# A mixture-of-experts tile's first weights: loaded from memory into a ring of four instead of copied on chip into a ring of three

## What is computed

```python
probs = jax.nn.softmax(x_flat @ w_gate + b_gate, axis=-1)      # 8 experts
route_p, route_idx = jnp.max(probs, axis=-1), jnp.argmax(probs, axis=-1)
h = jax.nn.relu(jnp.einsum('nd,edm->enm', x_flat, W1) + b1[:, None, :])   # 128 -> 512
y = jnp.einsum('enm,emd->end', h, W2) + b2[:, None, :]                    # 512 -> 128
out = y[route_idx, jnp.arange(n)] * route_p[:, None]
...
x = x + 0.5 * ffn(layernorm(x))
x = x + attn(layernorm(x))        # 16 heads of 8, causal
x = x + 0.5 * ffn(layernorm(x))
```

## Time and profile before

| | |
|---|---|
| runs | 321.22, 322.14, 323.71 us; median 322.14 |
| span of the profiled execution, first to last instruction | 319.3 us |
| TensorE busy | 276.5 us (87%) |
| VectorE busy | 214.5 us (67%) |
| ScalarE, GpSimd busy | 159.7 (50%), 178.8 us (56%) |
| DMA, mean over the span | 92 GB/s, 29.37 MB |
| expert tiles, first hidden product to last output product | 41.6 to 86 us and 264.4 to 309 us |

### The profile page before, as it was taken

How to read it: one execution, slowest core, us unless ns; L and a number is a source line. 1 busy time by engine, 2 the same in 40 slices (tenths; PEclk the granted TensorE clock), 3 DMA queues, 4 the chain that set the end, 5 groups by cost and what they waited for, 6 DMA issues and landing times.

```text
span 319.3 us, 7990 instructions
## 1 busy us (share of the span) xinstructions
PE 276.5 (87%) x2396; PEld 224.1 (70%) x2396; DVE 214.5 (67%) x691; ACT 159.7 (50%) x389; POOL 178.8 (56%) x319
## 2 busy tenths in 40 slices
PE   8573999999995776999999999998977699999960
PEld 8463999999994363656666566665646588999960
DVE  3877048788608759987666777776787555888850
ACT  2430076666204834586666667768541107666620
POOL 5577815554525201587777787788657730554551
PEclk9855999999999998799999999999976579999996
DMA  6973141220040731662524522110001143222100
GB/s 180 403 293 119 53 95 54 65 63 31 24 126 8 199 121 53 197 180 88 156 79 134 152 72 74 57 53 6 3 19 42 42 121 86 51 67 71 34 10 0
DMA packets 34387, 29.37 MB, mean 92 GB/s; under 512 B 4108, under 2 KB 28817, under 8 KB 34352
## 3 DMA queue, kind: packets, MB, share of 16 engines
q1 hardware_dynamic: 29696, 23.52, 24.6%
q0 software_dynamic: 2496, 4.27, 4.1%
q10 hardware_dynamic: 2160, 1.14, 1.4%
HBM read 17.08 MB, written 12.55 MB: 93 GB/s over the span
## 4 chain that ended last, share of the span: by engine, by line
PE 58%; POOL 11%; DVE 10%; issue 7%; DMA 5%; ACT 4%; POOLq 1%; ACTq 0%; SPq 0%; DVEq 0%
PE bank L1279 13%; PE bank L1290 12%; PE bank L1207 5%; PE bank L1436 3%; PE bank L1408 3%; PE bank L1384 3%; POOL pT L541 2%; POOL row L454 2%; PE bank L1381 2%; PE bank L1414 2%; PE bank L1271 2%; POOL disp_d L462 2%; PE bank L1240 2%; PE bank L1466 2%; PE bank L1389 1%
## 5 line engine op out<-in xcount | busy, mean ns | idle before, releaser
L723 ACT ACTIVATE pT<-bank 128x512 f32<-128x512 f32 x96 | 56.4, 599 | 36.2 <-PE bank L1414 25.2
L1207 PE MATMUL bank<-zero 128*128 128x128 f32 x298 | 43.2, 314 | 9.4 <-DVE rowi L916 4.7
L1279 PE MATMUL bank<-xsT,ew 128*128 128x128 f32 x368 | 48.8, 276 | 0.2
L1290 PE MATMUL bank<-experts,hT 128*128 x368 | 48.9, 276 | 0.0
L1207 PEld LDWEIGHTS bank<-zero 128*128 128x128 f32 x298 | 41.6, 227 | 10.1 <-DVE rowi L916 4.7
L1038 DVE TENSOR_REDUCE mh<-bank 128x2 f32<-128x512 f32 x64 | 42.1, 682 | 8.5 <-PE bank L1384 8.2
L541 POOL TENSOR_SCALAR_AFFINE_SELECT pT<-pT 128x512 f32<-128x512 f32 x62 | 39.8, 643 | 10.2 <-ACT pT L723 9.9
L1279 PEld LDWEIGHTS bank<-xsT,ew 128*128 128x128 f32 x368 | 44.7, 192 | 0.7 <-ACT xsT L621 0.3
L1290 PEld LDWEIGHTS bank<-experts,hT 128*128 128x128 f32 x368 | 44.8, 192 | 0.5 <-issue 0.3
L627 ACT ACTIVATE hT<-bank,ew 128x128 f32<-128x128 f32 x92 | 28.8, 364 | 28.9 <-PE bank L1279 28.9
L923 DVE TENSOR_SCALAR hT<-bank,ew 128x128 f32<-128x128 f32 x92 | 28.0, 346 | 20.2 <-PE bank L1279 18.9
(11 more groups left out here) (133 smaller groups left out, 479.4 us busy)
## 6 DMA issues: line engine op xcount, KB each, us to landing
sp_d<-spl SPq DMA_DIRECT2D x32, 192.0 KB, 2.6
experts<-in_experts SPq DMA_DIRECT2D x8, 578.0 KB
qz<-sp_d SPq DMA_DIRECT2D x32, 96.0 KB
ks<-sp_d SPq DMA_DIRECT2D x32, 96.0 KB
xs_sb<-disp_d SPq DMA_DIRECT2D x46, 66.0 KB, 1.8
row<-in_x SPq DMA_DIRECT2D x4, 256.0 KB, 5.5
row<-x_d SPq DMA_DIRECT2D x4, 256.0 KB, 5.0
disp_d<-pad ACTq DMA_DIRECT2D x12, 66.0 KB, 2.3
```

The lines of the kernel that those rows point to most:

```text
L723: act.activation(pT[:, u, :], bank[2 + u % 2][:, :], ACT.Exp, scale=SCALE).then_inc(a_e, 1)
L1207: pe.matmul(bank[b][:, 0:P], zero[:, :], zero[:, :], start=True, stop=True)
L1279: mm = pe.matmul(bank[2 + 2 * (k % 2) + c // 2][:, (c % 2) * P:(c % 2 + 1) * P], ew[:, k % WRING, c * P:(c + 1) * P], xsT[:, k % 2, :], st ...
L1290: mm = pe.matmul(bank[6 + k % 2][:, 0:D], hT[:, k % 2, c, :], w2.rearrange("p a c -> p (a c)"), start=(c == 0), stop=(c == HC - 1))
```

## The change

The ring `ew` gets four buffers. VectorE no longer copies into it. Instead SP loads a tile's W1, b1 and b2, 128 rows of 2,576 bytes (330 KB), straight from the input in memory, with the expert's number in a register. Four tiles' weights are loaded as soon as the tile table's `te` is there, ahead of the wait for dispatch; then twelve tiles' tokens; then, in turn, the weights of tile t (once the biasing of tile t-4 has freed the buffer) and the tokens of tile t+8 (once the scatter of tile t-4 has landed). Since several loads may be under way, `e_w` becomes four semaphores, one for each buffer, and ScalarE and VectorE wait for it as well as TensorE. Only W2 stays resident: 8 loads of 512 columns in place of 1,156. TensorE itself waits for the table and for W2 ahead of its first tile.

```diff
-WRING = 3
+WRING = 4
...
-        experts = sb("experts", [P, NE, ECOLS])
+        w2 = sb("w2", [P, NE, HC * D])
...
-        e_w = sems("expert_weights_copied", 2)
+        e_w = sems("expert_weights_loaded", WRING)
...
+        def weights_in(f, t):
+
+            return 16 * (f * len(range(t % WRING, NS, WRING)) + t // WRING + 1)
+
...
-                sp.dma_start(experts[:, e, :], experts_in[e * P:(e + 1) * P, :]).then_inc(e_all, 16)
+                sp.dma_start(w2[:, e, :], experts_in[e * P:(e + 1) * P, WCOLS:ECOLS]).then_inc(e_all, 16)
...
             def tile_loads(f):
 
-                sp.wait_ge(r_row, f + 1)
-                rows_ = loaded(mybir.EngineType.SP, rowi[0:1, 0:4], REGIONS + 1 - P)
-                sp.wait_ge(d_tok[f], 16 * NT)
-                sp.wait_ge(d_pad[f], 16 * NE)
-                for t in range(NS):
+                def tokens(t):
                     if t >= RING:
                         sp.wait_ge(e_st[(t - RING) % OUT], scattered(f, (t - RING) % OUT, (t - RING) // OUT + 1))
                     sp.dma_start(xs_sb[:, t % RING, :], disp_d[f][bass.ds(rows_[t % 4], P), :]
                                  ).then_inc(e_xs[t % RING], 16)
+
+                def weights(t):
+
+                    need(sp, e_yb[f], t - WRING + 1)
+                    if f:
+                        need(sp, e_yb[0], NS if t < WRING else 0)
+                    sp.dma_start(ew[:, t % WRING, :], experts_in[bass.ds(te_[t % 4] * P, P), 0:WCOLS]
+                                 ).then_inc(e_w[t % WRING], 16)
+
+                def rows_of(t):
+                    return loaded(mybir.EngineType.SP, rowi[0:1, t:min(t + 4, NS)], REGIONS + 1 - P)
+
+                def experts_of(t):
+                    return loaded(mybir.EngineType.SP, te[0:1, t:min(t + 4, NS)], NE - 1)
+                sp.wait_ge(r_te, f + 1)
+                te_ = experts_of(0)
+                for t in range(WRING):
+                    weights(t)
+                sp.wait_ge(r_row, f + 1)
+                rows_ = rows_of(0)
+                sp.wait_ge(d_tok[f], 16 * NT)
+                sp.wait_ge(d_pad[f], 16 * NE)
+                for t in range(RING):
+                    tokens(t)
                     if t % 4 == 3:
-                        rows_ = loaded(mybir.EngineType.SP, rowi[0:1, t + 1:min(t + 5, NS)], REGIONS + 1 - P)
+                        rows_ = rows_of(t + 1)
+                for t in range(WRING, NS):
+                    if t % 4 == 0:
+                        te_ = experts_of(t)
+                    weights(t)
+                    if t + RING - WRING < NS:
+                        if (t + RING - WRING) % 4 == 0 and t > WRING:
+                            rows_ = rows_of(t + RING - WRING)
+                        tokens(t + RING - WRING)
...
                 def relu(t, par, k):
                     act.wait_ge(e_h[f], t + 1)
+                    act.wait_ge(e_w[t % WRING], weights_in(f, t))
...
-                def weights(t, k):
-
-                    need(dve, e_yb[f], t - WRING + 1)
-                    dve.tensor_scalar(ew[:, k, :],
-                                      experts[:, bass.ds(te_[t % 4], 1), 0:WCOLS].rearrange("p a c -> p (a c)"),
-                                      1.0, None, ALU.mult).then_inc(e_w[f], 1)
-
...
-                    if t + WRING < NS:
-                        if (t + WRING) % 4 == 0:
-                            te_ = loaded(mybir.EngineType.DVE, te[0:1, t + WRING:min(t + WRING + 4, NS)], NE - 1)
-                        weights(t + WRING, t % WRING)
...
                 def hidden(t, i, k):
                     pe.wait_ge(e_Tc[f], t + 1)
-                    pe.wait_ge(e_w[f], t + 1)
+                    pe.wait_ge(e_w[t % WRING], weights_in(f, t))
...
+                pe.wait_ge(r_te, f + 1)
+                pe.wait_ge(e_all, 16 * NE)
                 turn(0)
```

More of the change, by code:

```diff
@@ L920, in relu @@
                     dve.wait_ge(e_h[f], t + 1)
+                    dve.wait_ge(e_w[t % WRING], weights_in(f, t))
                     need(dve, e_y[f], t - 1)
@@ L948, in scale @@
                                              xs_sb[:, k, 0:D], ALU.mult, ALU.add).then_inc(e_yc[f], 1)
[L950 to L954, removed]
                 relu(0, 0, 0)
@@ L1288, in output @@
                     for c in range(HC):
-                        w2 = experts[:, bass.ds(e, 1), WCOLS + c * D:WCOLS + (c + 1) * D]
+                        w2_e = w2[:, bass.ds(e, 1), c * D:(c + 1) * D]
                         mm = pe.matmul(bank[6 + k % 2][:, 0:D], hT[:, k % 2, c, :],
-                                       w2.rearrange("p a c -> p (a c)"), start=(c == 0), stop=(c == HC - 1))
+                                       w2_e.rearrange("p a c -> p (a c)"), start=(c == 0), stop=(c == HC - 1))
                     mm.then_inc(e_y[f], 1)
+                pe.wait_ge(r_te, f + 1)
+                pe.wait_ge(e_all, 16 * NE)
                 turn(0)
```

## The result

The change makes the kernel slower: 371.99 us median of six runs (368.73 to 376.70), beside 322.02 us (321.15 to 323.80) for the kernel before on the same chip. The ratio is 1.1498, interval 1.1453 to 1.1543, which is 48 us more. The forecast of 355 us had the direction and most of the mechanism, but 33 us were expected, and 370.4 lies at the very top of the range from 344 to 371.

The account below looks back on a forecast made before the run. TensorE was taken to set the pace in the expert stages. Stalls and register loads, 2 x (13.1 + 0.7), plus 1.0 us late start and 4 us of clock falls, added 32.6 to 322.1: 355 us, range 344 to 371.

Parts of the forecast that it names:

- once in three tiles: Expert stages, tiles 5, 8, 11 and 14: TensorE stalls 3.27 us each, the two tiles behind finding their weights ready.
- the copies are worth about 0: VectorE, expert stages: removing 46 copies of 0.49 us, none on the path, was taken to gain 0.
- three terms of the loop: Loop through SP from hidden(t) to hidden(t+3): products 1.96 us, scatter landing 2.4 and weights landing 2.5, within 8.95.
- register loads: SP's reads of experts' numbers before tiles 8 and 12, counted at 0.7 us a stage.
- The upper ends, 2.9 and 3.2: Loop through SP: the longest landings allowed, 2.9 us for a scatter and 3.2 for weights, making a loop of 10.15.
- the start of stage two: Between table and first tile of stage two: tokens issued later and queued behind 1.32 MB of weights, 1.0 us (0.6 to 1.5).
- No stall, with 0.7 us to spare: After tile 15, weights wait only for biasing of t-4: ready 3.0 us after output(t-4), needed at 3.7.
- two falls, 4 us: TensorE's clock falling to half in two of eight stalls, up to 1.8 us each, 4 us in the sum.
- the clock fell in most stalls: Rival for the expert stages: clock falls in most of eight stalls, 365 us (360 to 370), chance 0.17.
- transfers got in each other's way: Rival: weights share DMA engines with scatters and tokens; 361 us, up to 375 with clock falls, chance 0.13.
- The forecast's own case: Stalls in both expert stages with none to three falls of the clock, 347 to 360 us, chance 0.60.
- a mean of 160 GB/s: Argument against the transfers rival: 330 + 66 + 64 KB a tile in 2.9 us, of 416 GB/s seen.

Follow-up runs that it names:

- the 133 KB loads: The changed kernel with weight loads cut to 260 of 644 columns, all four hidden products using that quarter, so output differs: 359.26 us, ratio 1.1130.

## Why the prediction was right or wrong

**Right: the place and the cause.** The weights stand behind a wait for another transfer; with that wait taken away, 37 of 48 us go. In stage two TensorE stalled at 5, 8, 11 and 14 and nowhere else in the loop. In the first stage it stalled at these (2.58, 2.76, 1.44 and 1.29 us), but also at 10 and 13 (1.70 and 2.66 us), and for 0.3 to 0.8 us at 4, 7, 9, 12 and 15: the tiles behind a stalled one did not always find their weights ready, as the step "once in three tiles" had it. None is worth the name from 16 on (0.56 us once). SP's queue moved 36.06 MB after 23.52 (12.54 more, 12.5 expected), and the copies are worth about 0.

**Too small: three terms of the loop.** The six loops of the trace after, by the forecast's steps, in us: the products up to the end of output(t-1), bias and scaling up to the scatter's start, the scatter up to the issue of tokens, from there to the issue of weights, and the weights up to hidden(t+3):

| loop | products | to the scatter | scatter | to the weights' issue | weights | sum |
|---|---|---|---|---|---|---|
| forecast | 1.96 | 1.37 | 2.50 | 0.52 | 2.60 | 8.95 |
| stage one, 5 to 8 | 3.36 | 1.36 | 2.41 | 0.84 | 3.09 | 11.06 |
| 8 to 11 | 2.02 | 1.36 | 3.12 | 0.53 | 2.82 | 9.85 |
| 11 to 14 | 2.03 | 1.35 | 3.85 | 0.53 | 3.02 | 10.78 |
| stage two, 5 to 8 | 3.52 | 1.39 | 4.00 | 0.85 | 2.95 | 12.71 |
| 8 to 11 | 3.76 | 1.38 | 2.32 | 0.53 | 3.26 | 11.25 |
| 11 to 14 | 3.57 | 1.39 | 2.36 | 0.53 | 3.40 | 11.25 |

Together they are 13.2 us longer than six times 8.95. The largest part, 6.5 us, is in the products: they took 3.4 to 3.8 us in the four loops in which the clock had fallen, and 2.0 in the other two. The weights have 2.9 us of it, in every loop, and the scatter 3.1, from three loops of six; the other three scatters landed as fast as forecast. The longest of these scatters is the one at 307.0 us with no load beside it. The remaining 0.7 are register loads, which the forecast had beside the loop, at 0.7 a stage.

I had taken each landing by itself, from rows in which nothing like the other was in the air, and those rows hold fewer landings than their titles say: the trace of before has 8 of the first stage's scatters, 16 of all 46 and 22 of the 46 token loads. The upper ends, 2.9 and 3.2, were nearer. On the weights the Trainium skill's DMA: Bandwidth & Descriptors, section on the anatomy of one DMA, was nearer than I: its fit of 2.0 us plus bytes over 436 GB/s, which it gives for a DMA issued by GpSimd, makes an estimate of 2.76, where these loads by SP took 3.1 in the median. For the 133 KB loads it gives an estimate of 2.31, and the trace has 2.2.

**Too small: the start of stage two.** Forecast 1.0 us, measured 5.2. The timeline from 278 us:

```profile
278.26 0.95 POOL L494 DMA_INDIRECT disp_d<-row,slot  x1 [0.30 <-issue]
279.27 1.99 SPq L370 DMA_DIRECT2D ew<-in_experts  x4
282.21 6.28 SPq L362 DMA_DIRECT2D xs_sb<-disp_d  x11
286.86 0.88 ACT L647 ACTIVATE xq<-xs_sb 128x128 f32<-128x128 f32 x2 [12.82 <-DMA xs_sb<-disp_d]
```

From the last dispatch to the first tokens' issue it is 3.95 us (before: 258.29 to 261.27, 2.98), and these tokens took 4.6 us to land, not 1.8, behind 1.32 MB of weights: 3.8 us together. Then, behind 3.69 us in which TensorE had had nothing to do, the clock was at 0.50 from 288.8 to 292.2; the trace of before has no fall at this place. My sum had the bytes ahead of the tokens, but let them begin to flow from 260 on, and priced no fall of the clock there. With only two weight loads ahead and tokens before the others, 3.5 of the 5.2 us go.

**Too optimistic: "No stall, with 0.7 us to spare".** That held from tile 16 on, where no tokens are loaded. In the loop, with the wait for scatters gone, it did not: 3.9 us a stage, until the ring had six buffers. The 0.7 was counted on a landing of 2.5; a landing of 3.2 uses it up.

**The clock: the size right, the count wrong.** I took two falls, 4 us. There were six: one in the first stage (53.2 to 56.6), one at the start of stage two and one in each of its four stalls. A fall lengthened the products of its loop by 1.4 to 1.8 us, the forecast's size. Idle products in the stalls gave 5.7 us back, net of their own price. One-us windows at the stalls of tiles 5 and 8 of stage two (TensorE busy and products, further engines, granted clock, DMA share, GB/s), and each whole stage:

```profile
302.00:303.00 1.00, 0.85 (x5) 0.89 (x6) 0.00 (x0) 0.00 (x0) 0.00 (x0) 0.70 0.81 191
314.00:315.00 1.00, 0.15 (x1) 0.18 (x2) 0.00 (x0) 0.00 (x0) 0.00 (x0) 0.50 0.74 168
...
41.00:104.00 63.00, 47.88 (x387) 45.16 (x388) 25.88 (x90) 28.19 (x90) 19.88 (x21) 0.97 0.49 138
288.00:360.00 72.00, 55.75 (x390) 53.60 (x389) 26.57 (x92) 28.14 (x90) 19.80 (x21) 0.83 0.40 117
```

At 0.50 (1.2 GHz) hidden and output lie in the loop and lengthen it. The second stage lost 25.5 us and the first 18.8; its three further falls, at 1.4 to 1.8 us each, make some 5 of these 6.7 us. The Trainium skill's TensorE: Matmul & The Clock Gate, section on HAM oscillation, has a kernel that waits for a load between groups of products throttled in each wait. Stage two agrees with it (idle 3.51, 5.15, 3.12 and 3.24 us, four falls), stage one, with shorter waits, in one of three: idle 2.76 and 2.66 us kept 1.00, and 2.58 did not.

**The rivals.** Two of them came true together: the clock fell in most stalls of one stage, and transfers got in each other's way in both. The forecast's own case ended at 360, and the time is 370: that the range holds it, by less than 1 us, is owed to the room left for these two rivals, and the edge was luck. I gave these cases too little chance, since I counted them one at a time, though longer landings made longer stalls, and the four stalls above 3 us all came with a fall. Traffic was dismissed by a mean of 160 GB/s; the measured mean of stage one is lower, 138, and single scatters still took 3.0 to 4.1 us.

**Open.** How a scatter and a weight load slow each other on the DMA engines: shown is only that scatters which start close to a load land later, and less so when the load has fewer bytes. Whether the instruction packets make scatters late. And whether a ring of six for the weights alone, with tokens still twelve ahead, would have hidden the wait: that was not run.

## What to carry to other kernels

A load that is put into an in-order queue inherits every wait in front of it, also those written for other data, and a wait that costs nothing can become the bound: ask for each transfer whose wait it stands behind, and whether that wait is needed at that depth (eight tiles ahead in place of twelve was 37 us here). Price a transfer in a loop beside what will be in the air with it, and give a ring the depth of the landing under that traffic (six, not four). And look first whether the engine that is to be relieved bounds anything: here a second copy of everything cost 1.9 us.

## What was not expected of the hardware

- A scatter of 64 KB that landed in 2.2 to 2.6 us by itself took 3.0 to 4.0 when one 330 KB load was issued within 0.6 us of it, and 2.3 to 2.9 beside one of 133 KB, though the DMA engines were about half busy over the stage (share 0.49).
- With no load of SP beside it, a scatter took up to 4.0 us (299.3 us of the trace before). That trace has the landing of 16 scatters; the five that took 2.8 to 4.2 us all have an instruction packet in their flight; whether it is the cause is open.
- Idle times of 2.66 and 2.76 us before a product left the granted clock at 1.00 and one of 2.58 us did not, so the length of the gap alone did not decide.
